# A convolution and quantized FFN kernel: half of the early PSUM evacuations move from VectorE to ScalarE and GpSimd, with new orders of work in the opening

## The chip, the cores and the metric

One core of one Trainium2 chip. The metric is device microseconds of the kernel, median over runs. A profile of one execution comes with it; its times are read from the start of the span.

## What is computed

`x` is 128 samples x 32 channels x 512 positions, float32. A grouped convolution along the positions (4 groups of 8 channels, 9 taps, padding 4) plus a shift per sample and channel gives `y`. Each token (one sample, one channel) is then a row of 512 values for a feed-forward block whose operands are all rounded to 8 bits with a scale per row:

```python
out = lax.conv_general_dilated(x, weight, (1,), [(4, 4)], feature_group_count=4, ...)
y = out + einsum('nd,od->no', c, c_weight)[:, :, None] + bias[None, :, None]
gate = qlinear(y, w_gate)          # 512 -> 1376, both operands rounded per row
up = qlinear(y, w_up)
h = silu(gate) * up
x = x + qlinear(h, w_down)         # 1376 -> 512
```

`qlinear` takes max|row|/127 as a scale for each token and each weight row, rounds, and multiplies back.

## The kernel before

The samples lie on the 128 partitions. One **tile** is one channel: 128 tokens; there are 32 tiles. Each engine runs a program of its own, in an order written out by hand; semaphores are the only ties.

**Convolution.** A group of 8 channels is computed in 8 **spans** of 64 positions (q = 0 to 31; q = 8g + i). `conv_span(q)` (L743) issues five float32 matmuls per span, each two passes in the trace: stationary a block of `x`, moving a table `toeplitz`. They add into one PSUM bank of 8 x 64 values. The first block covers 16 positions, the next three 24, and the last one 8, which the constant `LEAST = 16` widens to 16 with zero taps, so 128 columns. `add_shift(q)` (L585) on VectorE reads the bank, adds the shift and writes `y`; every second span `fold_y(q)` (L597) reduces two spans to maxima. After the 8 spans of a group `group_top/scale/inverse` give the token scales `x_scale` and `x_inv`.

**Weights.** Eleven tiles of 128 rows of gate and up weights (`load_w`): VectorE takes maxima (`weights_top`, L561), scales and inverses; GpSimd rounds (`round_w`, L389, two instructions per tile); TensorE transposes (`turn_gate_up`, L764); ScalarE copies out of PSUM (`copy_gate_up`, L472). The scales are spread over partitions by `turn_xq` (L782) and `copy_xq`. The inverses are made in pairs of tiles, so GpSimd rounds in pairs. `round_y(0)` and `round_y(1)` feed the first two tokens tiles through TensorE.

**Opening.** Spans 0 to 11 (`FRONT = 12`) and the eleven weight tiles are done before tile 0, interleaved on TensorE as span q, weight tile q - 2.

**The tile loop.** Gate and up have 1376 columns in pieces of 512, 512 and 352. For piece p of tile i: TensorE `gate_or_up`; VectorE `scale_gate(i,p)` (L662); ScalarE `silu(i,p)` (L518); GpSimd `scale_silu(i,p)` (L429); VectorE `multiply_up(i,p)` (L672), which also frees the PSUM bank of `up`. The orders within tile i:

- VectorE: scale_gate(i,0), multiply_up(i-1,2), scale_gate(i,1), token_scales(i-1), multiply_up(i,0), scale_down, scale_gate(i,2), add_shift, multiply_up(i,1), folds, weights_down.
- ScalarE: silu(i,0), silu(i,1), round_down, round_y, round_h(i-1), silu(i,2), convert_h(i-1).
- GpSimd: scale_silu(i,0), add_residual, scale_silu(i,1), convert_y (L411), convert_down (L402), scale_silu(i,2).
- TensorE: two gate pieces, one up piece, down(i-5), span, the other three pieces.

`SPANS_AT` places spans 12 to 15 in tiles 0 to 3 and the rest in tiles 5 to 12 and 17 to 20. `CHANNELS_AT` places the rounding of tokens; `w_down` is rounded in tiles 0 to 3. SyncE's queue (its order is that of the program) turns `hq` by DMA, loads slabs 2 and 3 of `x_blocks` in iterations 4 and 5, and behind them the first residuals (L299), for which `add_residual(0)` waits in tile 6.

Of the kernel before, what the change touches and what calls it, by code (L numbers as in the profile page):

```python
# [5 lines left out]
ALU = mybir.AluOpType  # L6
# [6 lines left out]
P = 128  # L13
# [11 lines left out]
def adaln_ffn(nc, x, x_blocks, cond_ctx_bias, taps_wide, w_gate_up, w_down, out):  # L25
# [17 lines left out]
    LEAST = 16  # L43
# [17 lines left out]
    with ExitStack() as ctx:  # L61
# [94 lines left out]


        def halves(bank):
# [13 lines left out]
        y_ready = sem("y_ready")  # L172
        y_part_ready = sem("y_part_ready")
# [50 lines left out]
                   ("scales", 2, 0), ("scales", 2, 1)]  # L224
        BY_PE = 2

        def use(kind, part, m):
            return XQ_USES.index((kind, part, m))

# [6 lines left out]
                       for first, c, n in ((0, BY_PE, CI - BY_PE), (4, 8, CI), (13, 16, CI), (21, 24, CI))  # L236
# [7 lines left out]


# [6 lines left out]
        def _(sp):  # L252
# [77 lines left out]
            load_w(0)  # L330
            load_x_piece(0)
            load_w(1)
            load_x_piece(1)
            load_w(2)
            load_w(3)
            load_x_piece(2)
            load_w(4)
# [4 lines left out]
            load_slab(1, 0)  # L342
            load_slab(1, 1)
            for o in range(KT):
                load_w_down(o)
# [34 lines left out]
        def _(pool):  # L380
# [58 lines left out]
            for i in range(TILES):  # L439
# [6 lines left out]
                for o in down_at(i - 1):  # L446
                    convert_down(o)
                scale_silu(i, 2)
# [4 lines left out]
        def _(act):  # L453
            act.dma_start(small_sb[:, :], cond_ctx_bias).then_inc(small_in, 16)
            act.dma_start(toeplitz[:, :, :, :].rearrange("p g c o -> p (g c o)"), taps_wide).then_inc(taps_in, 16)

            act.wait_ge(small_in, 16)
            act.activation(silu_trial[:, :], small_sb[:, 0:1], ACT.Silu)

# [20 lines left out]
            def copy_xq(n):  # L480
                kind, part, m = XQ_USES[n]
                act.wait_ge(xq_turned, n + 1)
                bank = xq_bank[n % 2]
# [12 lines left out]
            for j in range(5):  # L496
                copy_gate_up(j)
            copy_xq(0)
            copy_xq(1)
            copy_gate_up(5)  # L500
            copy_gate_up(6)
# [3 lines left out]
            copy_xq(2)  # L505
            copy_xq(3)
            copy_xq(4)
            copy_gate_up(8)
            copy_gate_up(9)
            copy_xq(5)  # L510
            copy_gate_up(10)
# [20 lines left out]
            for i in range(TILES):  # L532
# [6 lines left out]
                for n in CHANNELS_AT.get(i, []):  # L539
                    round_y(n)  # L540
                if i:
# [8 lines left out]
        def _(dve):  # L550
# [399 lines left out]
```

## Time and profile before

| | |
|---|---|
| median of 3 runs | 312.16 us (311.69 to 314.09) |
| profiled execution | 311.69 us, its span 309.9 us |
| mean granted TensorE clock | 0.994 |
| TensorE matmul busy | 286.2 us (92%) |
| VectorE busy | 257.2 us (83%) |
| ScalarE busy | 190.1 us (61%) |
| GpSimd busy | 187.2 us (60%) |

The busy times are sums over stages with different limits, so what a change of one stage is worth has to be read in that stage. TensorE's matmul time is modelled and includes the pipeline's tail.

### The profile page before, as it was taken

To read this page: it belongs to the slowest core of one execution; us is meant where nothing else is said; L and a number is where in the kernel's file an instruction comes from. 1 tells how busy PE (TensorE), PEld (TensorE's weight loads), DVE (VectorE), ACT (ScalarE), POOL (GpSimd) and SP (SyncE) were. 2 spreads that over 40 slices of the span, in tenths; PEclk is the share of its full clock that TensorE was granted. 3 is DMA by queue.
4 is the path that set the end of the run, shared out by engine and by line. 5 is a ranking of instruction groups with operands and counts; after the bars stand their busy time and mean duration, and the time that the engine had idled before them with its cause. 6 is when DMAs were issued, how large, how long until landed. Compare 5 with 4: busy or idle time off the path is not lost.

```text
span 309.9 us, 4607 instructions
## 1 busy us (share of the span) xinstructions
PE 286.2 (92%) x1575; PEld 168.3 (54%) x1575; DVE 257.2 (83%) x419; ACT 190.1 (61%) x217; POOL 187.2 (60%) x195
## 2 busy tenths in 40 slices
PE   0997878879799999999999999999999999999995
PEld 0987855444455555555444466566444444444543
DVE  1699669999886988897998869888988888888863
ACT  1044765797974856555688835445688866676750
POOL 1354528676745766556598855346587766666653
PEclk9999999979999999999999999999999999999999
DMA  7999503347999864443278983453366665424336
GB/s 274 419 399 401 241 1 79 76 99 160 314 364 182 192 156 114 114 109 94 75 149 228 296 218 101 104 84 101 85 151 175 164 175 124 81 80 111 86 82 215
DMA packets 80390, 51.71 MB, mean 167 GB/s; under 512 B 69520, under 2 KB 69904, under 8 KB 79472
## 3 DMA queue, kind: packets, MB, share of 16 engines
q1 hardware_dynamic: 80080, 50.80, 59.4%
q10 hardware_dynamic: 288, 0.62, 0.7%
q8 instruction: 12, 0.20, 0.3%
q14 instruction: 10, 0.08, 0.1%
HBM read 26.12 MB, written 8.39 MB: 111 GB/s over the span
## 4 chain that ended last, share of the span: by engine, by line
PE 63%; DVE 18%; DMA 6%; ACT 4%; issue 4%; POOL 3%; SPq 1%; DVEq 0%; POOLq 0%
PE bank L852 35%; PE bank L869 16%; PE bank L759 10%; DVE h_mem L672 4%; DMA xo_mem<-x 3%; DVE h_max L678 3%; DVE gu_max L564 3%; DMA slab<-x_blocks 2%; DVE y_part L601 2%; DVE sg_mem L662 2%; POOL sg_mem L429 2%; DVE y_mem L592 2%; DMA hq_mem<-hq_mem 1%; DVE d_max L580 1%; ACT wgu_t L476 1%
## 5 line engine op out<-in xcount | busy, mean ns | idle before, releaser
L852 PE MATMUL bank<-wgu_t,xq_mem 128*128 128x512 bf16 (+1 forms) x768 | 157.1, 360 | 9.3 <-DVE h_mem L672 6.9
L429 POOL TENSOR_TENSOR sg_mem<-sg_mem,gu_scale_row 128x512 f32<-128x512 f32 (+1 forms) x96 | 111.3, 1162 | 85.0 <-ACT sg_mem L518 84.7
L852 PEld LDWEIGHTS bank<-wgu_t,xq_mem 128*128 128x128 bf16 x768 | 74.7, 98 | 82.8 <-DVE h_mem L672 10.8
L518 ACT ACTIVATE sg_mem<-sg_mem,x_scale 128x512 f32<-128x512 f32 (+1 forms) x96 | 64.8, 676 | 65.6 <-DVE sg_mem L662 65.3
L662 DVE TENSOR_TENSOR sg_mem<-bank,gu_scale_row 128x512 f32<-128x512 f32 (+1 forms) x96 | 60.1, 627 | 23.5 <-PE bank L852 23.5
L869 PE MATMUL bank<-wd_t,hq_mem 128*128 128x512 bf16 (+1 forms) x341 | 78.2, 379 | 0.0
L672 DVE SCALAR_TENSOR_TENSOR h_mem<-bank,x_scale,sg_mem 128x512 f32<-128x512 f32 (+1 forms) x96 | 66.3, 691 | 7.7 <-POOL sg_mem L429 6.8
L523 ACT ACTIVATE h_mem<-h_mem,h_inv 128x1376 f32<-128x1376 f32 x32 | 46.1, 1441 | 21.0 <-DVE h_inv L557 21.0
L759 PE MATMUL bank<-toeplitz,slab 128*128 128x192 f32 (+1 forms) x320 | 52.7, 317 | 4.8 <-DMA slab<-x_blocks 4.8
L759 PEld LDWEIGHTS bank<-toeplitz,slab 128*128 128x128 f32 x320 | 51.3, 199 | 7.4 <-DMA toeplitz<-taps_wide 3.0
L869 PEld LDWEIGHTS bank<-wd_t,hq_mem 128*128 128x128 bf16 (+1 forms) x341 | 33.3, 98 | 40.2 <-issue 0.3
L678 DVE TENSOR_REDUCE h_max<-h_mem 128x1 f32<-128x1376 f32 x32 | 50.4, 1575 | 0.0
L530 ACT ACTIVATE hq_mem<-h_mem 128x1376 bf16<-128x1376 f32 x32 | 42.7, 1334 | 0.0
L437 POOL TENSOR_TENSOR xo_mem<-xo_mem,hq_mem 128x512 f32<-128x512 f32 x24 | 30.5, 1270 | 3.7 <-DMA xo_mem<-x 3.7
L690 DVE SCALAR_TENSOR_TENSOR hq_mem<-bank,h_scale,wd_scale_row 128x512 f32<-128x512 f32 x31 | 23.0, 743 | 3.7 <-PE bank L869 3.7
L476 ACT ACTIVATE wgu_t<-bank 128x1024 bf16<-128x1024 int16 (+1 forms) x11 | 11.0, 1003 | 20.8 <-PE bank L772 20.8
L394 POOL TENSOR_SCALAR hq_mem<-hq_mem,gu_inv 128x512 f32<-128x512 f32 (+1 forms) x14 | 9.4, 691 | 14.4 <-DVE gu_inv L576 14.3
L592 DVE TENSOR_TENSOR y_mem<-bank,shift 128x512 f32<-128x512 f32 x24 | 15.9, 679 | 1.2 <-PE bank L759 1.2
L464 ACT ACTIVATE y_mem<-y_mem,x_inv 128x512 f32<-128x512 f32 x24 | 15.8, 707 | 0.1
L564 DVE TENSOR_REDUCE gu_max<-hq_mem 128x2 f32<-128x1024 f32 (+1 forms) x7 | 8.4, 1203 | 7.5 <-DMA hq_mem<-w_gate_up 7.5
L601 DVE TENSOR_REDUCE y_part<-y_mem 128x8 f32<-128x1024 f32 x12 | 14.5, 1210 | 0.0
L411 POOL TENSOR_SCALAR yq_mem<-y_mem 128x512 bf16<-128x512 f32 x22 | 13.3, 617 | 1.6 <-ACT y_mem L464 1.1
(54 smaller groups left out, 108.1 us busy)
## 6 DMA issues: line engine op xcount, KB each, us to landing
xo_mem<-x SPq DMA_DIRECT2D x24, 256.0 KB, 3.0
out<-xo_mem SPq DMA_DIRECT2D x24, 256.0 KB, 2.0
slab<-x_blocks SPq DMA_DIRECT2D x3, 1088.0 KB, 7.7
hq_mem<-w_gate_up SPq DMA_DIRECT2D x6, 512.0 KB, 8.7
slab<-x_blocks SPq DMA_DIRECT2D x3, 1024.0 KB, 10.2
slab<-w_down SPq DMA_DIRECT2D x3, 688.0 KB, 7.8
h_mem<-w_gate_up SPq DMA_DIRECT2D x4, 512.0 KB, 13.9
slab<-x SPq DMA_DIRECT2D x1, 2048.0 KB, 9.1
```

Source lines behind the costliest of these rows:

```text
L429: pool.tensor_tensor(s, s, gu_scale_row[:, 1, at:at + n], ALU.mult).then_inc(silu_scaled, 1)
L437: pool.tensor_tensor(xo_of(i), xo_of(i), down_out[:, i % 2, :], ALU.add).then_inc(out_ready, 1)
L518: act.activation(s, s, ACT.Silu, scale=x_scale[:, i:i + 1]).then_inc(silu_done, 1)
L523: act.activation(hi, hi, ACT.Copy, bias=MAGIC, scale=h_inv[:, i:i + 1]).then_inc(h_rounded, 1)
L530: act.activation(hq[i % HQ_BUFS][:, 0:INTER], h[i % H_BUFS], ACT.Copy, bias=-MAGIC).then_inc(hq_ready, 1)
L662: dve.tensor_tensor(sg[i % SG_BUFS][:, at:at + n], gate_bank[(NP * i + p) % 2][:, 0:n], gu_scale_row[:, 0, at:at + n], ALU.mult).then_inc( ...
L672: dve.scalar_tensor_tensor(h[i % H_BUFS][:, at:at + n], up_bank[(NP * i + p) % 2][:, 0:n], x_scale[:, i:i + 1], sg[i % SG_BUFS][:, at:at + ...
L678: dve.tensor_reduce(h_max[:, one], h[i % H_BUFS], AX_X, ALU.max, apply_absolute_value=True)\
L690: dve.scalar_tensor_tensor(down_out[:, i % 2, :], down_bank[i % 2][:, :], h_scale[:, i:i + 1], wd_scale_row[:, :], ALU.mult, ALU.mult).the ...
L759: last = pe.matmul(out_span[:, :, lo:hi], slabs[g % 2][:, PER_SPAN * i + b, :], toeplitz[:, g, :, tap:tap + hi - lo], start=(b == 0), stop ...
L852: last = pe.matmul(bank[n % 2][:, 0:cols], xq_t[:, g, k, P * c:P * (c + 1)], wgu_t[:, m, k, at:at + cols], start=(k == 0), stop=(k == KT - 1))
L869: last = pe.matmul(down_bank[i % 2][:, :], hq_t[i % HQT_BUFS][0:r, j, :], wd_t[0:r, j, :], start=(j == 0), stop=(j == JT - 1))
```

## The change

- **Evacuation split.** Spans 2 to 5 and 8 to 15 (`BY_ACT`, twelve spans) are no longer evacuated by `add_shift`. ScalarE copies the bank to `y` (`copy_span`), GpSimd adds the shift in place (`shift_span`), and `fold_y` waits for GpSimd.
- **Placement.** GpSimd shifts spans 2, 3 after rounding weight tile 3, spans 4, 5 after tile 5, and spans 8 to 15 in tiles 0 to 4 ahead of `scale_silu(i,2)` (`SHIFTS_AT`). The folds of group 1 move to tiles 3 to 5 (`FOLDS_AT`), the tokens of group 1 from tiles 4 to 7 to tiles 6 to 9.
- **Opening.** TensorE's, VectorE's and ScalarE's orders are written out anew. Spans 8 to 11 come behind weight tile 7. Weight tile 10 and the last two spreads of scales move into tile 0, behind its first two gate pieces, which wait only for eight weight tiles.
- **Loads.** `w` tile 1 goes ahead of the first piece of `x`, other pieces change places; the taps are loaded in two parts, the second after weight tile 5 has landed; three of the four `w_down` tiles go ahead of the second half of slab 1.
- **Narrow last blocks.** `LEAST` is 8: the last block of each span has 64 columns in place of 128, and the table of taps shrinks by a quarter.

The core of the diff:

```diff
-    LEAST = 16
+    LEAST = 2 * PAD
+        BY_ACT = [2, 3, 4, 5] + list(range(SPANS, 2 * SPANS))
+        BY_DVE = [q for q in range(SLOTS) if q not in BY_ACT]
-                       for first, c, n in ((0, BY_PE, CI - BY_PE), (4, 8, CI), (13, 16, CI), (21, 24, CI))
+                       for first, c, n in ((0, BY_PE, CI - BY_PE), (6, 8, CI), (13, 16, CI), (21, 24, CI))
+        SHIFTS_AT = {0: [8], 1: [9], 2: [10, 11], 3: [12, 13], 4: [14, 15]}
+        FOLDS_AT = {3: [9, 11], 4: [13], 5: [15]}
+        def conv_bank_free(engine, q):
+            if q in BY_ACT:
+                engine.wait_ge(conv_copied, BY_ACT.index(q) + 1)
+            else:
+                engine.wait_ge(y_ready, BY_DVE.index(q) + 1)
...
+            load_w(1)
             load_x_piece(0)
-            load_w(1)
+            load_w(2)
             load_x_piece(1)
...
+            def shift_span(q):
+                g, i = divmod(q, SPANS)
+                span = y[g][:, :, SPAN * i:SPAN * (i + 1)]
+                pool.wait_ge(shift_ready, 1)
+                pool.wait_ge(conv_copied, BY_ACT.index(q) + 1)
+                pool.tensor_tensor(span, span, shift[:, CI * g:CI * (g + 1)].unsqueeze(2).broadcast_to([P, CI, SPAN]),
+                                   ALU.add).then_inc(y_shifted, 1)
+
             for j in range(JT):
                 round_w(j)
+                if j == 3:
+                    shift_span(2)
+                    shift_span(3)
+                elif j == 5:
+                    shift_span(4)
+                    shift_span(5)
...
                 for o in down_at(i - 1):
                     convert_down(o)
+                for q in SHIFTS_AT.get(i, []):
+                    shift_span(q)
                 scale_silu(i, 2)
...
+            act.wait_ge(w_tile_in[5], 16)
+            act.dma_start(toeplitz[:, 1:GROUPS, :, :]..., taps_wide[:, group_taps:]).then_inc(taps_rest_in, 16)
+            def copy_span(q):
+                g, i = divmod(q, SPANS)
+                act.wait_ge(conv_done, q + 1)
+                act.activation(y[g][:, :, SPAN * i:SPAN * (i + 1)],
+                               conv_bank(q)[:, :].rearrange("p (c l) -> p c l", c=CI), ACT.Copy).then_inc(conv_copied, 1)
...
# VectorE, the opening's new order
+            weights_inverse(0, 2)
+            weights_top(2)
             add_shift(0)
+            add_shift(1)
+            weights_top(3)
+            weights_scale(2, 2)
+            fold_y(1)
+            weights_inverse(2, 2)
+            weights_top(4)
+            weights_top(5)
+            weights_scale(4, 2)
+            fold_y(3)
+            weights_inverse(4, 2)
+            weights_top(6)
+            add_shift(6)
+            weights_top(7)
             add_shift(7)
+            weights_scale(6, 2)
+            fold_y(5)
+            weights_inverse(6, 2)
+            fold_y(7)
...
# TensorE, the opening's new order
+            turn_gate_up(0)
+            turn_gate_up(1)
+            conv_span(2)
+            conv_span(3)
+            turn_gate_up(2)
+            conv_span(4)
+            conv_span(5)
+            turn_gate_up(3)
+            turn_xq(0)
+            turn_xq(1)
+            conv_span(6)
+            conv_span(7)
+            turn_gate_up(4)
+            turn_gate_up(5)
+            turn_xq(2)
+            turn_xq(3)
+            turn_gate_up(6)
+            turn_gate_up(7)
+            turn_xq(4)
+            conv_span(8)
+            conv_span(9)
+            turn_gate_up(8)
+            conv_span(10)
+            turn_gate_up(9)
+            conv_span(11)
...
                 gate_or_up(i, 0, 1)
+                if i == 0:
+                    turn_gate_up(10)
+                    turn_xq(5)
+                    turn_xq(6)
                 gate_or_up(i, 1, 0)
```

ScalarE's new order in the opening is copies of weight tiles 0 and 1, spans 2 and 3, weight tiles 2 and 3, spans 4 and 5, scales, weight tiles 4 and 5, scales, weight tile 6, `round_y(0)` and `(1)`, weight tile 7, the first tokens, spans 8 and 9, then weight tiles 8, 9 and 10 among spans 10 and 11 and the last scales. In tiles 0 to 3 it copies spans 12 to 15 ahead of `round_h`.

## Rows read from the trace of the kernel before

**Rows 1.** Two stretches: busy us (instructions) by engine, clock, DMA share, GB/s.
```profile
60.00:80.00 20.00, 15.72 (x76) 8.03 (x77) 19.62 (x35) 17.00 (x20) 14.35 (x14) 0.91 0.68 154
...
99.00:146.00 47.00, 46.79 (x250) 27.51 (x251) 41.72 (x67) 27.62 (x30) 29.68 (x28) 1.00 0.52 130
```

**Rows 2.** Chain that ended last, 41 to 100 us: start us, us, what.
```profile
85.47 10.23 DMA xo_mem<-x
```

**Rows 3.** VectorE timeline, opening: start, us, engine, line, operation, count, idle before.
```profile
13.36 0.69 DVE L592 TENSOR_TENSOR y_mem<-bank,shift 128x512 f32<-128x512 f32 x1 [0.46 <-PE bank L759]
```

**Rows 4.** GpSimd timeline of the opening, same columns.
```profile
16.75 2.69 POOL L394 TENSOR_SCALAR hq_mem<-hq_mem,gu_inv 128x512 f32<-128x512 f32 x4 [2.15 <-DVE gu_inv L576]
...
21.65 2.69 POOL L394 TENSOR_SCALAR hq_mem<-hq_mem,gu_inv 128x512 f32<-128x512 f32 x4 [2.21 <-DVE gu_inv L576]
...
34.47 1.35 POOL L394 TENSOR_SCALAR hq_mem<-hq_mem,gu_inv 96x512 f32<-96x512 f32 x2
```

**Rows 5.** TensorE timeline of the opening, same columns.
```profile
7.79 6.95 PE L759 MATMUL bank<-toeplitz,slab 128*128 128x128 f32 x30 [2.85 <-DMA slab<-x_blocks]
...
28.39 1.69 PE L759 MATMUL bank<-toeplitz,slab 128*128 128x128 f32 x10 [1.96 <-DMA slab<-x_blocks]
...
34.49 0.62 PE L804 MATMUL bank<-ident_bf,y_mem 128*128 128x128 bf16 x8 [1.16 <-ACT gu_scale_row L486]
...
41.48 2.76 PE L852 MATMUL bank<-wgu_t,xq_mem 128*128 128x512 bf16 x12 [1.58 <-ACT gu_scale_row L486]
```

**Rows 6.** Groups by shape, first 70 us: busy us, mean ns, idle.
```profile
L429 POOL TENSOR_TENSOR sg_mem<-sg_mem,gu_scale_row 128x512 f32<-128x512 f32 x8 | 10.0, 1274 | 9.5 <-ACT sg_mem L518 9.5
...
L601 DVE TENSOR_REDUCE y_part<-y_mem 128x8 f32<-128x1024 f32 x4 | 4.8, 1212 | 0.0
...
L411 POOL TENSOR_SCALAR yq_mem<-y_mem 128x512 bf16<-128x512 f32 x6 | 3.7, 617 | 1.1 <-ACT y_mem L464 1.1
...
L486 ACT ACTIVATE gu_scale_row<-bank 128x512 f32<-128x512 f32 x4 | 2.2, 594 | 0.0
...
L796 PEld LDWEIGHTS bank<-ident,gu_scale 128*128 128x128 f32 x20 | 2.1, 137 | 0.0
```

**Rows 7.** ScalarE timeline: first two SiLUs, then the second of tiles 1 to 5.
```profile
43.77 1.34 ACT L518 ACTIVATE sg_mem<-sg_mem,x_scale 128x512 f32<-128x512 f32 x2 [2.34 <-DVE sg_mem L662]
...
52.05 0.72 ACT L518 ACTIVATE sg_mem<-sg_mem,x_scale 128x512 f32<-128x512 f32 x1 [0.36 <-DVE sg_mem L662]
...
60.98 0.72 ACT L518 ACTIVATE sg_mem<-sg_mem,x_scale 128x512 f32<-128x512 f32 x1 [0.37 <-DVE sg_mem L662]
...
68.79 0.72 ACT L518 ACTIVATE sg_mem<-sg_mem,x_scale 128x512 f32<-128x512 f32 x1 [0.37 <-DVE sg_mem L662]
...
76.50 0.72 ACT L518 ACTIVATE sg_mem<-sg_mem,x_scale 128x512 f32<-128x512 f32 x1 [0.37 <-DVE sg_mem L662]
...
83.11 0.72 ACT L518 ACTIVATE sg_mem<-sg_mem,x_scale 128x512 f32<-128x512 f32 x1 [0.52 <-DVE sg_mem L662]
```

**Rows 8.** GpSimd timeline, last SiLU product of tile 2.
```profile
66.23 0.94 POOL L429 TENSOR_TENSOR sg_mem<-sg_mem,gu_scale_row 128x352 f32<-128x352 f32 x1
```

**Rows 9.** VectorE timeline, the `up` product behind it.
```profile
67.58 0.57 DVE L672 SCALAR_TENSOR_TENSOR h_mem<-bank,x_scale,sg_mem 128x352 f32<-128x352 f32 x1
```

**Rows 10.** TensorE timeline of tiles 1 to 7.
```profile
54.62 3.36 PE L852 MATMUL bank<-wgu_t,xq_mem 128*128 128x352 bf16 x16 [1.43 <-DVE h_mem L672]
...
63.55 5.04 PE L852 MATMUL bank<-wgu_t,xq_mem 128*128 128x352 bf16 x16 [2.00 <-DVE h_mem L672]
...
99.21 1.04 PE L852 MATMUL bank<-wgu_t,xq_mem 128*128 128x512 bf16 x4 [0.73 <-DVE h_mem L672]
```

**Rows 11.** Groups by line and shape, 155 to 281 us.
```profile
L759 PEld LDWEIGHTS bank<-toeplitz,slab 128*128 128x128 f32 x80 | 12.0, 191 | 0.6
...
L759 PE MATMUL bank<-toeplitz,slab 128*128 128x192 f32 x48 | 9.1, 326 | 0.0
...
L759 PE MATMUL bank<-toeplitz,slab 128*128 128x128 f32 x32 | 5.5, 274 | 0.0
```

More of the change, by code:

```diff
@@ L342, in _ @@
             load_slab(1, 0)
+            for o in range(KT - 1):
+                load_w_down(o)
             load_slab(1, 1)
-            for o in range(KT):
-                load_w_down(o)
+            load_w_down(KT - 1)
             for i in range(TILES + 1):
@@ L494, in copy_down_row @@
                 act.activation(wd_scale_row[:, :], down_bank[1][:, :], ACT.Copy).then_inc(wd_row_copied, 1)
-            for j in range(5):
-                copy_gate_up(j)
+            copy_gate_up(0)
+            copy_gate_up(1)
+            copy_span(2)
+            copy_span(3)
+            copy_gate_up(2)
+            copy_gate_up(3)
+            copy_span(4)
+            copy_span(5)
             copy_xq(0)
             copy_xq(1)
+            copy_gate_up(4)
             copy_gate_up(5)
+            copy_xq(2)
+            copy_xq(3)
             copy_gate_up(6)
@@ L540, in _ @@
                     round_y(n)
+                for q in SPANS_AT.get(i, []):
+                    if q in BY_ACT:
+                        copy_span(q)
                 if i:
@@ L704, in _ @@
                 for q in SPANS_AT.get(i, []):
-                    add_shift(q)
+                    if q in BY_DVE:
+                        add_shift(q)
                 multiply_up(i, 1)
-                for q in SPANS_AT.get(i, []):
-                    if q % 2:
-                        fold_y(q)
+                for q in FOLDS_AT.get(i, []):
+                    fold_y(q)
                     if q % SPANS == SPANS - 1:
@@ L809, in turn_down_row @@
                 pe.wait_ge(d_scale_ready, KT)
-                pe.wait_ge(y_ready, FRONT)
+                pe.wait_ge(xq_copied, use("scales", 2, 1) + 1)
                 spread(down_bank[1], lambda t: d_scale[:, t:t + 1], KT).then_inc(wd_row_turned, 1)
@@ L846, in gate_or_up @@
                 else:
-                    pe.wait_ge(xq_copied, len(XQ_USES))
+                    pe.wait_ge(xq_copied, use("tokens", 0, 0) + 1)
+                    pe.wait_ge(w_copied, ROW_PARTS[p][1])
+                if n == 2:
                     pe.wait_ge(w_copied, JT)
@@ L860, in down @@
                         pe.wait_ge(wd_turned[b], 16 * KT // WDQ_BUFS)
-                    pe.wait_ge(y_ready, FRONT)
+                    pe.wait_ge(xq_copied, use("scales", 2, 0) + 1)
                 elif i == 1:
```

92 lines of the change are left out of this document (41 added, 51 removed).

## The prediction

> **What bounds the kernel now.** The table of stretches comes first: it says which engine is full where. From 99 us on TensorE is busy without a gap (46.79 of 47.00 us), while between 60 and 80 us it is VectorE that is full, 19.62 of 20.00 us, and GpSimd has 14.35 [rows 1]. So the run has three parts: an opening up to the first gate piece at 41.48 us [rows 5], tiles 0 to 4 with VectorE full, and from tile 5 on TensorE's own pace, which takes over each microsecond that the first two parts win or lose. Late in the second part the chain of waits leaves the engines: the first residual lands 10.23 us after its issue at 85.47 [rows 2], and TensorE stands still for 0.73 us before 99.21 because of it [rows 10]. Next the timelines of the opening, engine by engine, and then the SiLUs of the tiles, because the loop VectorE, ScalarE, GpSimd, VectorE shows in them as one beat per tile [rows 7].
>
> **Opening, what is removed.** VectorE gives up eight shifts (spans 2 to 5, 8 to 11) and two folds of 1.21 us (mean 1212 ns, [rows 6]) before tile 0. It gets a head start on the weights as well, since tile 1 now lands ahead of `x`. But it can't use it: `add_shift(1)` still stands ahead of `weights_top(3)`, and the second span ends when it did, because the first spans start on the first piece of `x` (7.79 us, [rows 5]; 512 KB of weights go ahead, some 400 KB of taps go behind, so the same time), and `add_shift(1)` at 13.36 was already waiting for TensorE [rows 3]. From there on the same four operations follow as before, so GpSimd gets the inverses of weight tiles 2 and 3 at about the 16.75 us of now [rows 4].
>
> **Opening, what is added.** From there each pair of weight tiles goes through a ring of waits: GpSimd rounds the pair (2.69 us, [rows 4]), then does two shifts; VectorE waits in `fold_y` for the second, folds (1.21), and only behind that stands `weights_inverse` of the next pair, for which GpSimd waits. The price of a shift is not in the trace. It is a two-input float32 operation of 512 elements; the nearest row is the SiLU product on the same engine with 1274 ns, started every 1.24 us; the one-input conversion has 617 ns [rows 6]. I take 1.24, because two inputs are what they share, and keep 0.62 as the lower end; nothing shows an upper end above 1.3. The ring is then 2.69 + 2.5 + 1.2 + 0.3 of handoffs = 6.7 us against 21.65 - 16.75 = 4.9 us now [rows 4]. Pair 4, 5 starts at 23.4, pair 6, 7 at 30.1, pair 8, 9 at 34.7 (behind `fold_y(7)`, the group's scales and two maxima), tile 10 ends at 38.8 where it now ends at 34.47 + 1.35 = 35.8 [rows 4].
>
> The Trainium skill (GPSIMD Engine Reference, The C++ chunk loop) says that both inputs of a two-input operation go through one read port, about 2.5 cycles per element at the least. The trace agrees, 1274 against 617 ns [rows 6]; by that page a broadcast second input saves nothing.
>
> TensorE turns weight tile 6 at 31.5, ScalarE copies it and rounds two channels, and the tokens are turned at 34.5, just as at 34.49 now [rows 5]. Behind this stand four spans, where two stood: 2 x 1.45 = 2.9 us more. Against them the wait of 1.58 us ahead of the first gate piece goes [rows 5], and weight tile 10 and two spreads (1.2 us) move behind it. First gate piece: 41.48 + 2.9 - 1.6 - 1.2 = 41.6. The first SiLU stands in ScalarE's queue behind the copies of what was moved: 41.6 + 1.7 (two gate pieces) + 1.2 + 1.7 (three copies with handoff) = 46.2, less 0.8 as the first copy starts while TensorE still spreads, so 45.4 against 43.77 [rows 7]. **Opening: +1.6 us.** ScalarE's eight copies of spans (594 ns each by the nearest PSUM copy, [rows 6]) lie in its idle time; without it they would cost 8 x 0.6 = 4.8. Its new wait for weight tile 5 holds up `copy_gate_up(0)` and all behind it by some 2 us; GpSimd asks for span 2 only after weight tile 3, so it costs nothing.
>
> **The clock.** In the new opening TensorE has nothing to do from 27.9 (scales spread) to 31.5 us (weight tile 6 rounded), then 0.9 us of transposes within 3 us, then the serial stretch that sets tile 0. Now it idles 1.96 us there [rows 5] and keeps its clock; but 2.00 us idle ahead of 63.55, in a stretch that was thin already, was followed by the lower level (1.2 GHz): the same 16 matmuls took 5.04 us in place of 3.36 [rows 10], +1.7 us. That drop was hidden by VectorE. Here it would be on the path. The idle time is nearly twice as long, so I count it: **+1.7 us**, bounds 0 and 3.4.
>
> **Tiles 0 to 4.** VectorE sheds four shifts (0.6 each) and its folds change places. GpSimd gets one, one, two, two and two shifts, each ahead of `scale_silu(i,2)`, and queued behind that on VectorE stand `multiply_up(i,2)`, then `scale_gate(i+1,1)`, `token_scales` and the rest; TensorE waits for the banks. So the beat counts. In tile 2 that product ends at 66.23 + 0.94 = 67.17 [rows 8] and VectorE takes it at 67.58 [rows 9]: 0.41 us of slack, for 2 x 1.24 = 2.5 us of new work, +2.05. The same reading of the other four tiles: tile 0, one shift against 0.35 slack and a ScalarE copy in the same queue, +1.15; tile 1, one shift against 1.55 slack, -0.2 (VectorE's saving shows); tile 3, two shifts against 1.6 slack, with two folds more on VectorE, +0.45; tile 4, two shifts, but two conversions of 0.6 leave GpSimd and ScalarE's `round_h` sets the end anyway, +0.15. **Sum +3.6 us**: the beats of now (44.40, 52.05, 60.98, 68.79, 76.50, 83.11; that is 7.65, 8.9, 7.8, 7.7, 6.6, [rows 7]) become 8.8, 8.7, 9.85, 8.15, 6.75. GpSimd is the bound in place of VectorE. At 0.62 per shift the sum would be +0.3, with VectorE the bound in tiles 3 and 4.
>
> **Tiles 5 on.** The residual's landing comes later by less than TensorE does, since slab 2 is out of its way by then: the 0.73 us [rows 10] goes, **-0.7**, bounds 0 and -0.7. The last fold of group 1 and its scales lengthen tile 5 to some 8.4 us of VectorE, no more than TensorE needs there (45 matmuls per tile, at 250 in 47.0 us [rows 1]: 8.46); its cost is 0, or 0.5 without that cover. The tokens of group 1 have two tiles of lead, cost 0.
>
> **Narrow last blocks.** 64 columns fewer save 326 - 274 = 52 ns per pass [rows 11], two passes, 0.105 us per span at most. But the next float32 weight load must be in by then. It has 191 ns [rows 11], a load with one spread column 137 [rows 6]: float32 loads of a full block are no shorter than the pass they hide under, so I let only the last pass of a span gain, and only where bf16 follows. That is twelve of the sixteen spans inside TensorE's stretch: **-0.65 us**, bounds 0 and -1.7. The Trainium skill (TensorE: Matmul & The Clock Gate, LDWEIGHTS) gives a load of 128 columns as 128/1.2 = 107 ns; by that rule the pass ahead of another float32 load gains nothing. No row shows a 64-column pass.
>
> **Sum.** 1.6 + 1.7 + 3.6 - 0.7 - 0.65 = +5.5 us on the profiled 311.69: 317.2. The median of the runs lies 0.47 above that execution, so 317.6.
>
> **Rivals.**
>
> 1. *The clock holds.* The same without 1.7: 315.9. For it: 1.96 us idle at 26.4 passed without a drop. Against: a longer gap.
> 2. *GpSimd's shift is cheap (0.62 us)*, a broadcast input costing like none. Ring 5.4 us, tokens turned 2.6 us earlier, the first SiLU 1.0 earlier than now; tiles +0.3; narrow blocks -0.65; the stall -0.1: 310.7. It decides below some 0.75 us per shift. Against: every two-input row of GpSimd.
> 3. *VectorE's relief comes through*, the other side. If the shifts fit GpSimd's idle 30 to 40% without ever being waited for, VectorE's twelve shifts of 0.6 come off a full engine: 312.2 - 7.2 - 0.65 = 304.3, less what TensorE takes up first, so 304 to 308. It decides where GpSimd's last SiLU product still ends before VectorE asks. Against: 0.41 us slack in tile 2.
> 4. *The split hangs on waits I placed too late*, 312 to 314: the opening turns even because the maxima run ahead, and only tile 2 loses.
>
> A measurement of this kernel tells 1% (3.1 us) from no change. Chances: forecast 0.37, rival 1 0.20, rival 2 0.13, rival 3 0.10, rival 4 0.20. Slower by over 1% means above 315.3: all of the forecast, most of rival 1: 0.53. Faster means below 309.0: rival 3 and a tail of 2: 0.15. Within: 0.32. The range leaves rival 3 and the far end of the bounds out: 309.5 to 319.8; the forecast's own is 316.3 to 319.5.
>
> **What would show it.** GpSimd's `shift_span` at 1.24 us; VectorE idle ahead of `fold_y(3)` and `fold_y(5)`, on GpSimd; rounding of pairs at 23.4 and 30.1 us; TensorE idle near 28 to 31.5 and a granted clock of 0.5 behind it; the first SiLU near 45.4 (47 with the drop); `multiply_up(2,2)` waiting for GpSimd some 2 to 3 us; the second SiLU of tile 5 near 88 to 90; a 10-pass span of 1.37 us where bf16 follows. A shift below 0.75 us, or VectorE with no idle time in tiles 2 and 3, would make me wrong.

## The result and the profile after

The changed kernel takes 316.63 us, the median of five runs (314.99 to 317.34), against 312.16 before: ratio 1.0116, 95% interval 1.0074 to 1.0158. It is slower, as forecast, by 1.2% in place of 1.7% (the two medians lie 1.4% apart). The profiled execution is the quickest of the five (314.99 us, span 313.2), so against the profiled one before it is 3.3 us longer.

The page's busy times and slices come first.

```profile
PE 287.7 (92%) x1575; PEld 168.4 (54%) x1575; DVE 252.0 (80%) x407; ACT 195.8 (63%) x229; POOL 199.5 (64%) x207
...
PEclk9999799979899999999999999999999999999999
```

VectorE lost 5.2 us of work and GpSimd gained 12.3, and the kernel is longer: a busy time that falls on a full engine is no gain when what it waits for comes later. The clock's row has three slices below 9, where that of before had one:

```profile
PEclk9999999979999999999999999999999999999999
```

The stretches of the changed kernel show where they lie (busy us and instructions by engine, clock, DMA share, GB/s).

```profile
30.00:41.00 11.00, 9.20 (x78) 8.88 (x77) 6.06 (x11) 7.73 (x10) 5.16 (x8) 0.84 0.56 232
...
60.00:80.00 20.00, 16.05 (x80) 8.47 (x78) 16.36 (x27) 15.43 (x19) 16.58 (x17) 0.91 0.55 116
80.00:99.00 19.00, 16.87 (x80) 9.06 (x80) 16.53 (x29) 11.45 (x15) 10.40 (x10) 0.91 1.11 330
```

VectorE is no longer full between 60 and 80 us: 16.36 us where it had 19.62 [rows 1]. Now the opening, first GpSimd's timeline, to be held against [rows 4].

```profile
16.12 2.71 POOL L415 TENSOR_SCALAR hq_mem<-hq_mem,gu_inv 128x512 f32<-128x512 f32 x4 [5.37 <-DVE gu_inv L638]
18.79 2.05 POOL L442 TENSOR_TENSOR y_mem<-y_mem,shift 128x512 f32<-128x512 f32 x2
22.27 2.70 POOL L415 TENSOR_SCALAR hq_mem<-hq_mem,gu_inv 128x512 f32<-128x512 f32 x4 [1.44 <-DVE gu_inv L638]
24.94 2.04 POOL L442 TENSOR_TENSOR y_mem<-y_mem,shift 128x512 f32<-128x512 f32 x2
28.42 2.70 POOL L415 TENSOR_SCALAR h_mem<-h_mem,gu_inv 128x512 f32<-128x512 f32 x4 [1.44 <-DVE gu_inv L638]
32.95 2.71 POOL L415 TENSOR_SCALAR h_mem<-h_mem,gu_inv 128x512 f32<-128x512 f32 x4 [1.83 <-DVE gu_inv L638]
```

The pairs of weight tiles are rounded from 16.12, 22.27 and 28.42 us on: the ring of 6.15 us. The idle time of 1.44 us before the second and third pair is on the inverse, which VectorE hasn't issued yet, as its timeline shows.

```profile
20.87 1.22 DVE L666 TENSOR_REDUCE y_part<-y_mem 128x8 f32<-128x1024 f32 x1 [2.02 <-POOL y_mem L442]
22.00 0.17 DVE L638 RECIPROCAL gu_inv<-gu_scale 128x4 f32<-128x4 f32 x1
```

`fold_y(3)` waits 2.02 us for GpSimd's shift, and the reciprocal behind it is what GpSimd waits for. TensorE's timeline of the opening and of the start of its own stretch, against [rows 5, 10]:

```profile
29.84 0.62 PE L842 MATMUL bank<-ident_bf,h_mem 128*128 128x128 bf16 x8 [1.63 <-POOL h_mem L415]
...
32.88 1.01 PE L877 MATMUL bank<-ident_bf,y_mem 128*128 128x128 bf16 x8 [1.08 <-ACT y_mem L512]
33.69 3.96 PE L829 MATMUL bank<-toeplitz,slab 128*128 128x128 f32 x20
...
41.23 1.89 PE L939 MATMUL bank<-wgu_t,xq_mem 128*128 128x512 bf16 x8
```

```profile
82.33 5.05 PE L939 MATMUL bank<-wgu_t,xq_mem 128*128 128x352 bf16 x16 [2.13 <-DVE h_mem L740]
...
89.60 1.53 PE L829 MATMUL bank<-toeplitz,slab 128*128 128x128 f32 x10
...
104.00 2.54 PE L956 MATMUL bank<-wd_t,hq_mem 128*128 128x512 bf16 x11
```

The same two places in TensorE's timeline of before:

```profile
79.10 3.36 PE L852 MATMUL bank<-wgu_t,xq_mem 128*128 128x352 bf16 x16 [2.03 <-DVE h_mem L672]
...
100.08 2.54 PE L869 MATMUL bank<-wd_t,hq_mem 128*128 128x512 bf16 x11
```

Spans 8 and 9 take 3.96 us from the first start to the last end (3.01 in experiments 2 to 4), and the 16 matmuls at the start of TensorE's stretch (82.33) 5.05 us where the same ones of before took 3.36. Part of each lies at the lower clock: the granted clock is 0.74 from 33.7 to 37.5 us and 0.65 from 82.3 to 87.2, where it was 1.00 over the 3.4 us from 79.0 of before. The SiLUs, against [rows 7]:

```profile
44.90 1.34 ACT L577 ACTIVATE sg_mem<-sg_mem,x_scale 128x512 f32<-128x512 f32 x2
```

```profile
54.01 0.72 ACT L577 ACTIVATE sg_mem<-sg_mem,x_scale 128x512 f32<-128x512 f32 x1 [1.64 <-DVE sg_mem L730]
...
62.52 0.72 ACT L577 ACTIVATE sg_mem<-sg_mem,x_scale 128x512 f32<-128x512 f32 x1 [1.08 <-DVE sg_mem L730]
...
72.02 0.72 ACT L577 ACTIVATE sg_mem<-sg_mem,x_scale 128x512 f32<-128x512 f32 x1 [2.08 <-DVE sg_mem L730]
...
79.74 0.72 ACT L577 ACTIVATE sg_mem<-sg_mem,x_scale 128x512 f32<-128x512 f32 x1 [0.49 <-DVE sg_mem L730]
...
86.90 0.72 ACT L577 ACTIVATE sg_mem<-sg_mem,x_scale 128x512 f32<-128x512 f32 x1 [0.99 <-DVE sg_mem L730]
```

The beats are 8.5, 9.5, 7.7 and 7.2 us between tiles 1 and 5. From the first SiLU to the second one of tile 5 it is 42.0 us, before 39.3. The product behind GpSimd's shifts in tile 2, against [rows 8, 9]:

```profile
67.76 2.04 POOL L442 TENSOR_TENSOR xq_mem<-xq_mem,shift 128x512 f32<-128x512 f32 x2
69.76 2.17 POOL L464 TENSOR_TENSOR sg_mem<-sg_mem,gu_scale_row 128x352 f32<-128x352 f32 x2
```

```profile
70.80 0.58 DVE L740 SCALAR_TENSOR_TENSOR h_mem<-bank,x_scale,sg_mem 128x352 f32<-128x352 f32 x1 [2.20 <-POOL sg_mem L464]
```

Two shifts end at 69.80, the product of 352 columns follows, and VectorE has been idle for 2.20 us when it can take it.

The account of the profiled span: TensorE's stretch begins 3.23 us later (82.33 against 79.10), of which 1.13 stand at the first SiLU (44.90 against 43.77). Its first 16 matmuls add 1.69. The wait of 0.73 us [rows 10] is gone; from start to start it had cost 0.90 (9.34 from one `down` to the next, now 8.39 with a span 0.05 shorter). With that and two narrow spans the changed kernel is 3.92 us behind when the third `down` of the stretch starts (104.00 against 100.08). Of these 0.64 are won back up to the last `down`: 0.54 by ten gains of 0.05 from the narrow blocks, 0.10 by a shorter last wait.

### The profile page after: what moved, and what is told of

It is laid out like the page before. It is cut to its first block, busy times and chain, and to the rows that moved or that the text cites. A ratio compares the mean times of both kernels' runs of the same rounds, so it can differ in the third digit from the quotient of the medians.

```text
span 313.2 us, 4635 instructions
## 1 busy us (share of the span) xinstructions
PE 287.7 (92%) x1575; PEld 168.4 (54%) x1575; DVE 252.0 (80%) x407; ACT 195.8 (63%) x229; POOL 199.5 (64%) x207
## 3 DMA queue, kind: packets, MB, share of 16 engines
HBM read 25.99 MB, written 8.39 MB: 110 GB/s over the span
## 4 chain that ended last, share of the span: by engine, by line
PE 68%; DVE 11%; POOL 8%; ACT 5%; issue 5%; DMA 3%; SPq 0%; DVEq 0%; POOLq 0%
PE bank L939 36%; PE bank L956 17%; PE bank L829 12%; POOL sg_mem L464 4%; DVE h_max L746 2%; DVE h_mem L740 2%; DMA slab<-x_blocks 2%; DVE sg_mem L730 2%; DVE y_part L666 1%; DMA hq_mem<-hq_mem 1%; POOL xq_mem L442 1%; ACT sg_mem L577 1%; PE bank L842 1%; ACT h_mem L582 1%; DVE y_mem L654 1%
## 5 line engine op out<-in xcount | busy, mean ns | idle before, releaser
L939 PE MATMUL bank<-wgu_t,xq_mem 128*128 128x512 bf16 (+1 forms) x768 | 159.2, 362 | 9.3 <-DVE h_mem L740 8.7
L829 PE MATMUL bank<-toeplitz,slab 128*128 128x192 f32 (+2 forms) x320 | 51.3, 314 | 2.9 <-DMA slab<-x_blocks 2.9
L654 DVE TENSOR_TENSOR y_mem<-bank,shift 128x512 f32<-128x512 f32 x20 | 13.3, 681 | 2.5 <-PE bank L829 2.5
```

The source lines that it names most:

```text
L829: last = pe.matmul(out_span[:, :, lo:hi], slabs[g % 2][:, PER_SPAN * i + b, :], toeplitz[:, g, :, tap:tap + hi - lo], start=(b == 0), stop ...
L939: last = pe.matmul(bank[n % 2][:, 0:cols], xq_t[:, g, k, P * c:P * (c + 1)], wgu_t[:, m, k, at:at + cols], start=(k == 0), stop=(k == KT - 1))
```

## The experiments

Each kernel is the changed one with one edit, unless said otherwise. Ratios are to the kernel before, run beside it; the changed kernel's is 1.0116, so 0.001 is 0.31 us. Differences from the changed kernel go by these ratios; its own, of five runs, is known to 1.3 us to each side.

Two things differ between executions of one kernel, and every profile below is one execution. One is the start: GpSimd's rounding of weight tiles 2 and 3, from which the ring runs, began at 16.12 us in the changed kernel's profile and at 15.88 to 17.10 in those of the experiments with the same opening up to there. The other is the clock: beside the experiments, 27 executions of the kernel before with a mean granted clock of 0.989 took 313.1 us on the average, and 29 with 0.993 or 0.994 took 311.7.

**1. The shifts of the tiles behind the last product.**

```diff
-                for q in SHIFTS_AT.get(i, []):
-                    shift_span(q)
                 scale_silu(i, 2)
+                for q in SHIFTS_AT.get(i, []):
+                    shift_span(q)
```

> The changed kernel with the eight shifts of tiles 0 to 4 behind the last SiLU product of their tile on GpSimd. Theory (the queue order: a shift ahead of that product holds up VectorE's up product): the waits of 1.2, 1.2 and 2.2 us go, the beats of the second SiLU fall from 8.5, 8.5, 9.5, 7.7 to about 7.7, 7.6, 7.6, 7.6, so the profiled span falls by 3 us, to 310.2 or below before. Rival A (the GpSimd work itself is too much, wherever it stands): within 1 us of the changed kernel. Rival B (only the lower TensorE clock costs): beats fall, but the time follows the number of clock drops alone.

Ratio 1.0028 (0.9999 to 1.0057): 2.7 us faster than the changed kernel with all its shifts still done. From the first SiLU to the second one of tile 5 it is 39.2 us, as before. ScalarE's timeline:

```profile
46.62 1.34 ACT L577 ACTIVATE sg_mem<-sg_mem,x_scale 128x512 f32<-128x512 f32 x2
...
54.74 0.72 ACT L577 ACTIVATE sg_mem<-sg_mem,x_scale 128x512 f32<-128x512 f32 x1 [0.65 <-DVE sg_mem L730]
...
62.65 0.72 ACT L577 ACTIVATE sg_mem<-sg_mem,x_scale 128x512 f32<-128x512 f32 x1 [0.49 <-DVE sg_mem L730]
...
70.56 0.72 ACT L577 ACTIVATE sg_mem<-sg_mem,x_scale 128x512 f32<-128x512 f32 x1 [0.49 <-DVE sg_mem L730]
...
85.80 0.72 ACT L577 ACTIVATE sg_mem<-sg_mem,x_scale 128x512 f32<-128x512 f32 x1 [0.98 <-DVE sg_mem L730]
```

That first SiLU is 1.7 us later than the changed kernel's: 1.0 because this execution started later, and 0.7 by a longer stretch at the lower clock in the opening.

```profile
17.10 2.71 POOL L415 TENSOR_SCALAR hq_mem<-hq_mem,gu_inv 128x512 f32<-128x512 f32 x4 [6.44 <-DVE gu_inv L638]
```

So its span, 312.0 us, hides part of the gain, and I missed the 310.2. Rival A is out: elsewhere in the queue the same work costs nothing against before, though VectorE's relief of four shifts doesn't show either. Rival B is out as well for the beats: both profiles have a granted clock of 0.982 and the drop at tile 5, and the beats fall. It is not out for the whole of the 2.7 us, since the runs of this kernel have clocks of 0.982 to 0.989 and those of the changed one 0.973 to 0.982; at 0.982 two runs took 313.7 us on the average and the one of the changed kernel 314.99. The first beats are near 7.9 us, 0.2 to 0.4 longer than I wrote.

**2. The inverses ahead of the folds.**

```diff
-            fold_y(3)
             weights_inverse(4, 2)
+            fold_y(3)
...
-            fold_y(5)
             weights_inverse(6, 2)
+            fold_y(5)
```

> The changed kernel with weights_inverse ahead of fold_y(3) and fold_y(5) in the opening. Theory (the ring of waits in the opening, GpSimd shift, fold, inverse, GpSimd rounding): pairs of weight tiles are rounded every 4.8 us (2.7 + 2.0 + handoff) in place of 6.15, the tokens are turned 1.5 to 2.5 us earlier than at 32.9, the first SiLU near 42.5 in place of 44.9: 2 us faster. Rival (TensorE's own work in the opening is what counts, the fold's wait is hidden): 0 to 0.5 us.

Ratio 0.9995 (0.9966 to 1.0024), 3.8 us faster: nearly twice what I expected of an exchange of two neighbours. GpSimd's and ScalarE's timelines:

```profile
20.57 2.72 POOL L415 TENSOR_SCALAR hq_mem<-hq_mem,gu_inv 128x512 f32<-128x512 f32 x4
...
26.37 2.70 POOL L415 TENSOR_SCALAR h_mem<-h_mem,gu_inv 128x512 f32<-128x512 f32 x4 [1.08 <-DVE gu_inv L638]
```

```profile
41.53 1.34 ACT L577 ACTIVATE sg_mem<-sg_mem,x_scale 128x512 f32<-128x512 f32 x2
```

The pair 4, 5 starts at 20.57, without any wait behind the shifts, and pair 6, 7 at 26.37. The first SiLU is at 41.53, 3.4 us ahead of the changed kernel's: 2.0 by the ring (tokens turned at 30.85), of which 0.2 lie in the start of this execution, and 1.3 because the tokens' transposes and spans 8 and 9 now find the high clock (3.01 us for the spans). The drop at tile 5 stays (5.05 us for the 16 matmuls). The rest of the 3.8 is within the intervals.

**3. and 4. Matmuls without use in TensorE's idle time.** Seventeen float32 ones in the opening (experiment 3), and the same with eight bf16 ones per tile in tiles 0 to 4 (experiment 4):

```diff
+            def keep_busy(n):
+                for _ in range(n):
+                    pe.matmul(banks[6][:, 0:P], ident[:, :], ident[:, :], start=True, stop=True)
...
+            pe.wait_ge(conv_copied, 3)
+            keep_busy(4)
             turn_xq(2)
             turn_xq(3)
+            keep_busy(6)
             turn_gate_up(6)
+            keep_busy(3)
             turn_gate_up(7)
+            keep_busy(4)
             turn_xq(4)
...
                 gate_or_up(i, 1, 1)
+                if i == 0:              # from here on experiment 4 only
+                    pe.wait_ge(xq_copied, use("scales", 2, 0) + 1)
+                if i < LAG:
+                    for _ in range(8):
+                        pe.matmul(down_bank[0][:, :], xq_t[:, 0, 0, 0:P], wgu_t[:, 0, 0, 0:512], start=True, stop=True)
                 gate_or_up(i, 1, 2)
```

> The changed kernel with 17 float32 matmuls without use put into TensorE's idle time between 26 and 33 us; they write a bank that the next span overwrites. Theory (the lower clock at 33 to 36 us comes from that idle time and is on the path): granted clock 1.00 up to 41 us, spans 8 and 9 in 2.8 in place of 3.8 us, first SiLU 1.0 us earlier, time 1 us lower. Rival (the drop is hidden, or comes whatever TensorE does): same time within 0.3 us.

> The same, and in tiles 0 to 4 eight more bf16 matmuls without use (1.7 us) ahead of the last up piece, where TensorE waits about 2 us. Theory: no stretch at the lower clock after 41 us either, tile 5's 16 matmuls in 3.4 in place of 5.05 us: 2.7 us faster than the changed kernel in all, and runs closer together (their clocks now differ from 0.973 to 0.982). Rival (tiles 0 to 4 are bound by GpSimd and VectorE so that a slower TensorE is hidden): no faster than with the opening alone.

Ratios 1.0029 (0.9998 to 1.006) and 1.0000 (0.9973 to 1.0026). In the first the spans 8 and 9 take 3.01 us, and with the tokens' transposes 1.3 us are won. This execution started 0.56 us later (16.68 in place of 16.12), and the extra matmuls put nothing off, so the first SiLU is at 44.14, 0.8 us earlier. The profiled spans differ by 1.2 us (312.0), since 0.7 of the lead of 1.9 at the first `down` is lost in the wait for the last turned `hq` (0.95 us in place of 0.24). The ratios differ by more: 2.7 us, with intervals of 1.0 and 1.3 us to each side. The stretch in which TensorE takes over, by its timeline in experiment 4:

```profile
33.67 3.01 PE L829 MATMUL bank<-toeplitz,slab 128*128 128x128 f32 x20
...
81.36 3.36 PE L948 MATMUL bank<-wgu_t,xq_mem 128*128 128x352 bf16 x16 [0.41 <-DVE h_mem L740]
```

```profile
core 0: 310.5 us, clock 1.000
```

16 matmuls in 3.36 us, and the granted clock is 1.000 over the whole run. The beats of tiles 1 to 4 stay what they were (8.5, 9.5 and 7.7 us), and only the one that ends in tile 5 falls, from 7.2 to 6.5 (43.91 to 85.23: 41.3 us in all), so the clock and GpSimd's queue are two costs and not one. The twelve runs lie within 311.45 to 312.96, the five of the changed kernel within 314.99 to 317.34 at clocks of 0.973 to 0.982; a stretch that adds 1.7 us, like that at tile 5, takes 0.0055 from the mean over 313 us. Which of these stretches fall on the path differs from run to run: the profile of experiment 3 has one at 55.82 us, where it was hidden, one at 73.84, where it cost 0.5 us (a beat of 8.3 in place of 7.7), and none at tile 5. With the tiles' idle time left as it is, a drop stands at tile 5 in the profiles of experiments 1, 2, 5, 9 and 11, and only earlier in those of 3, 6 and 8.

**5. VectorE takes spans 8 to 15 back.**

```diff
-        BY_ACT = [2, 3, 4, 5] + list(range(SPANS, 2 * SPANS))
+        BY_ACT = [2, 3, 4, 5]
...
-        SHIFTS_AT = {0: [8], 1: [9], 2: [10, 11], 3: [12, 13], 4: [14, 15]}
+        SHIFTS_AT = {}
...
-            copy_span(8)
-            copy_span(9)
             copy_gate_up(8)
-            copy_span(10)
             copy_gate_up(9)
-            copy_span(11)
...
             for o in down_at(-1):
                 weights_down(o)
+            for q in range(8, 12):
+                add_shift(q)
```

> The changed kernel with spans 8 to 15 evacuated by VectorE again: 8 to 11 behind its last weight work in the opening, where it now idles 6 us, 12 to 15 in tiles 0 to 3 as before; spans 2 to 5 stay split, the folds stay where the change put them. Theory (GpSimd's shifts ahead of the last product are what tiles 0 to 4 pay for): beats of the second SiLU 7.7, 7.8 to 8.0, 7.8, 8 to 9, 6.5 and the tiles 2 to 2.7 us shorter in sum. Rival A (VectorE is so full that its shifts cost as much as GpSimd's): no change within 1 us. Opening unchanged within 0.5 us by both, apart from clock drops.

Ratio 1.0040 (1.0019 to 1.0061), 2.4 us faster; 39.8 us from the first SiLU to the second of tile 5, beats 7.8, 7.8, 8.2 and 7.6. It has a drop at tile 5 too, as TensorE's timeline says:

```profile
79.97 5.04 PE L937 MATMUL bank<-wgu_t,xq_mem 128*128 128x352 bf16 x16 [2.03 <-DVE h_mem L738]
```

Against experiment 1 (39.2 us) this prices VectorE's own relief once GpSimd's queue is in order, in one execution of each: 0.6 us for four shifts, less than the 2.4 us they last. By their ratios the two kernels are 0.4 us apart, within the intervals.

**6. 128 columns again in the last block.**

```diff
-    LEAST = 2 * PAD
+    LEAST = 16
```

> The changed kernel with the last block of each span 128 columns wide again (and the table of taps as large as before). Theory (the last pass of a span gains only where a bf16 matmul follows): a span of ten passes 1.42 us again in place of 1.37, 2.84 in place of 2.79 for a pair, so the profiled span 0.6 us longer, within what a measurement tells. Rival (both passes of 64 columns gain): 0.105 us per span, 1.7 us longer. Rival (the loads gain too, by the smaller table): the first span starts later by over 0.3 us.

Ratio 1.0164 (1.0141 to 1.0187), 1.5 us slower than the changed kernel, but the two intervals overlap, so the time can't tell the 0.6 us of the theory from the 1.7 of the rival. The lengths can. Two spans in a row, by TensorE's timelines of the changed kernel and of this one:

```profile
185.07 2.95 PE L829 MATMUL bank<-toeplitz,slab 128*128 128x128 f32 x20
```

```profile
186.61 3.00 PE L829 MATMUL bank<-toeplitz,slab 128*128 128x128 f32 x20
```

A pair gains 0.05 us, as much as a single span (1.53 in place of 1.58), so the span that is followed by float32 gains nothing and the rival is out. The passes, in the groups by shape from 155 to 281 us of the changed kernel and of this one (busy us, mean ns, idle):

```profile
L829 PE MATMUL bank<-toeplitz,slab 128*128 128x64 f32 x16 | 2.6, 247 | 0.0
```

```profile
L829 PE MATMUL bank<-toeplitz,slab 128*128 128x128 f32 x32 | 5.5, 274 | 0.0
```

The 247 ns are a mean of two kinds of record: the first pass of a narrow block has 219 ns, and the second starts 56 ns behind it (273 and 109 with 128 columns); the second pass has 275 ns at either width, and bf16 follows 111 or 112 ns behind its start. Ahead of a float32 span the first pass of that span takes the 0.05 us again (165 ns to the next start in place of 112). So the gain shows in the first pass of the block and not in the last, and is kept only where bf16 follows.

**7. The narrow blocks alone**, on the kernel before.

> The kernel before with the narrow last blocks alone. Theory: ten passes of a span in 1.37 in place of 1.42 us where bf16 follows, in the sixteen spans inside TensorE's stretch and nowhere else on the path: 0.65 us faster at most, which a measurement hardly tells; taps that are a quarter smaller start the first span up to 0.3 us earlier. Rival (both passes gain): 1.7 us faster.

Ratio 0.9957 (0.9928 to 0.9985): 1.3 us faster. The first SiLU is at 43.13 in place of 43.77, but most of that is there before the opening's spans can have given it:

```profile
16.23 2.69 POOL L394 TENSOR_SCALAR hq_mem<-hq_mem,gu_inv 128x512 f32<-128x512 f32 x4 [2.36 <-DVE gu_inv L576]
```

Weight tiles 2 and 3 are rounded from 16.23 us on in place of 16.75 [rows 4], which a smaller table of taps may have given or the execution's luck. Behind the tokens' transposes only two spans are left, 0.1 us. TensorE's timeline shows a single span of 1.53 us in place of 1.58 from first start to last end.

```profile
81.67 2.54 PE L869 MATMUL bank<-wd_t,hq_mem 128*128 128x512 bf16 x11
```

The first `down` starts at 81.67, before at 82.29; the last one 1.70 us ahead of before's. In between are the twelve gains of 0.05 us (0.65, as worked out) and 0.4 by a shorter wait for the residual (0.29 us in place of 0.73). The measured 1.3 us has an interval that holds my 0.65, and the rival's 1.7 it doesn't exclude by itself, but the spans' length does (0.05 each, not 0.105).

**8. A full second input for the shift** (y + y in place of y + shift, so the shift itself is left out of the result).

```diff
-                pool.tensor_tensor(span, span, shift[...].unsqueeze(2).broadcast_to([P, CI, SPAN]),
+                pool.tensor_tensor(span, span, span,
```

> The changed kernel with the shift's broadcast operand replaced by the span itself (y + y in place of y + shift for the twelve spans; this part of the result is left wrong). It asks why a shift took 1.02 us where the SiLU product of the same size takes 1.24. Theory (a second input that is read from one address per channel is cheaper): 1.24 us each, and the time 1.5 to 2.5 us longer, since GpSimd's additions are on the path. Rival (the three-dimensional pattern or the in-place add makes it cheaper): 1.02 us again and no change in time.

Ratio 1.0156 (1.0131 to 1.0181), no slower than the changed kernel beyond the intervals, and the groups by shape up to 90 us, of the changed kernel and of this one, say why:

```profile
L442 POOL TENSOR_TENSOR xq_mem<-xq_mem,shift 128x512 f32<-128x512 f32 x8 | 8.2, 1043 | 0.0
```

```profile
L442 POOL TENSOR_TENSOR xq_mem<-xq_mem 128x512 f32<-128x512 f32 x8 | 8.2, 1040 | 0.0
```

1040 ns with two full inputs, 1043 with the broadcast one. My theory fell: the broadcast is not what makes the shift cheaper than a product of the same size.

**9. Both reorderings**, the edits of experiments 1 and 2 together.

> The changed kernel with both reorderings: GpSimd's shifts behind the last product of a tile, and weights_inverse ahead of fold_y(3) and fold_y(5). Theory (two separate places, so the gains add): 3.8 + 2.7 = 6.5 us faster than the changed kernel, near 310.2, 0.7% below before, less what a clock drop at tile 5 (1.7 us) takes back. Rival (one hidden behind the other, or behind the loads of slabs 2, 3 and the residuals): no better than the better one alone, 312.

Ratio 0.9908 (0.9888 to 0.9928), 309.57 us: the gains add (6.5 us by the ratios, as expected). TensorE's timeline still has the drop at tile 5:

```profile
76.94 5.05 PE L939 MATMUL bank<-wgu_t,xq_mem 128*128 128x352 bf16 x16 [2.03 <-DVE h_mem L740]
```

**10. The same with the matmuls without use in tiles 0 to 4.**

> The kernel with both reorderings, and eight bf16 matmuls without use per tile in tiles 0 to 4 ahead of the last up piece. Theory (the drop to the lower clock at tile 5 is on the path, 5.05 in place of 3.36 us for 16 matmuls, and follows from the idle time of tiles 0 to 4): granted clock 1.00 throughout, tile 5's matmuls in 3.4, 1.5 us faster than without, near 308.0. Rival (with VectorE the bound in tiles 0 to 4, the extra matmuls delay the last up piece): no change or slower by up to 1 us.

Ratio 0.9884 (0.9858 to 0.9911), 309.1 us. TensorE's timeline shows tile 5's 16 matmuls, and the last `down` of all; under it is the same last row of experiment 9:

```profile
77.24 3.35 PE L939 MATMUL bank<-wgu_t,xq_mem 128*128 128x352 bf16 x16
```

```profile
301.46 2.58 PE L998 MATMUL bank<-wd_t,hq_mem 128*128 128x256 bf16 x22 [1.08 <-DMA hq_mem<-hq_mem]
```

```profile
301.99 2.58 PE L993 MATMUL bank<-wd_t,hq_mem 128*128 128x256 bf16 x22 [0.23 <-DMA hq_mem<-hq_mem]
```

The 16 matmuls take 3.35 us, and the `down` of each tile starts 1.4 us ahead of experiment 9's (80.43 against 81.82 for the first). The last one starts only 0.5 us ahead: in the tail TensorE is not the bound, and it waits 1.08 us for the turned `hq` where it waited 0.23. So the 1.5 us I expected are there until the tail and 0.5 us at its end; the intervals of the two kernels overlap. Two of experiment 9's six runs had a clock of 1.000 without any such matmuls, and took 308.26 and 308.73 us.

**11. The product of GpSimd in the shift's pattern**, on the kernel of experiment 9.

```diff
-                pool.tensor_tensor(s, s, gu_scale_row[:, 1, at:at + n], ALU.mult)
+                s3 = s.rearrange("p (c l) -> p c l", c=CI)
+                pool.tensor_tensor(s3, s3, gu_scale_row[:, 1, at:at + n].rearrange("p (c l) -> p c l", c=CI), ALU.mult)
```

> The kernel with both reorderings and the SiLU product of GpSimd addressed as 8 rows of 64 (or 44) in place of 512 (352) elements in a row; the same elements. It asks why a shift takes 1.04 us and a product of the same size 1.27. Theory (the pattern in two dimensions is what makes it cheaper, since a shift with a full second input took 1.04 as well): 1.04 us a product, 5 to 8 us of GpSimd's busy time gone in all, total time at most 1 us lower as GpSimd is hidden for most of the run. Rival (the buffers, or the pattern is merged back when it is built): 1.27 again and no change.

Ratio 0.9877 (0.985 to 0.9904), no different from experiments 9 and 10. The product's row is what it was:

```profile
L465 POOL TENSOR_TENSOR sg_mem<-sg_mem,gu_scale_row 128x512 f32<-128x512 f32 x33 | 42.1, 1277 | 26.8 <-ACT sg_mem L579 26.8
```

The trace's own records say why: the product's operands stand there as one row of 512 elements (`[512,1,1]`), as in the other kernels, and the shift's as 8 rows of 64 (`[64,8,1]`). The pattern was merged back, the second rival, and this tried nothing new about the time.

## Why the prediction was right

**The ring of the opening** was right as a mechanism, and experiment 2 shows it: with the two instructions exchanged its first turn takes 4.7 us and the second 5.8, with 0 and 1.08 us of waiting. Its size was off by one term, the price of a shift: 1.02 us from start to start against my 1.24, so 6.15 us per turn against 6.7. I had 0.62 and 1.3 as ends and went by the nearest row, which was the wrong one by 0.2. Two turns of it make 1.1 us. The second span was done 0.6 us earlier than I took from [rows 3], which is luck of this execution: in the other profiles with this opening the ring starts 0.2 us earlier to 1.0 later. Together they had the tokens turned at 32.9, not 34.5. The first SiLU came 1.13 us later, of which the clock has 1.3: without it the opening of this execution would have cost nothing, not 1.6.

**The clock** came as forecast in the opening, and cost 1.3 us there, not 1.7. That the idle time brings it is shown by experiment 3, and by the profiles at large: the eight transposes of the tokens take 1.01 us in all five with this opening's waits (the changed kernel, experiments 1, 5, 6 and 8) and 0.61 in all six where the idle time is filled or shortened (experiments 2, 3, 4, 9, 10, 11). But the shape I gave was wrong: no gap of 3.6 us, but four of 1.14, 1.63, 0.72 and 1.08 between 26.0 and 32.9, none as long as the 1.96 of before or the 2.70 us of experiment 7 that passed without a drop. I compared the longest gap. The four together make 4.6 us; in experiment 2, where the clock held, they make 2.8. What I left out is the second drop, at tile 5, at the very place where TensorE takes over: 1.69 us in the profile, and gone in experiment 4. I had said of a drop in the tiles that VectorE hides it, going by the one at 63.55 [rows 10]; a hidden drop and one on the path differ only by which tile they fall in. The change is not its only cause: by their clocks, 0.005 lower, nearly half of the executions of the kernel before have one such stretch more than its profile, and are 1.5 us longer.

**Tiles 0 to 4**: +3.6 forecast; measured +2.1 up to the start of TensorE's stretch (3.23 less 1.13), +2.7 up to the second SiLU of tile 5, which already waits for TensorE at the lower clock. The order of the waits was right (experiments 1 and 5); the size was off by the same term: the first four beats (8.5, 8.5, 9.5, 7.7) came out 0.3, 0.2, 0.35 and 0.4 us below mine, with one, one, two and two shifts in them of 0.22 us less each. The two shifts of tile 4 cost nothing. The idle times I read are there: 1.2, 1.2 and 2.2 us ahead of `multiply_up(i,2)` in tiles 0 to 2.

**The residual's wait** went, -0.7 forecast and -0.9 from start to start. **The narrow blocks** gave 0.05 us at each of twelve places in TensorE's stretch, 0.65 as worked out, and for the reason given (only where bf16 follows), though the records show it in the first narrow pass and not in the last.

**The sum**, +5.5 against +3.3 in the profile, is the balance of errors of both signs: opening 1.8 and tiles 1.5 too dear, the clock 1.3 too cheap (3.0 in two drops), the last two terms 0.3 too small. That the total came within 1 us of the measured median is in part luck. The 0.47 us between the profiled execution and the median was a poor guide as well: the changed kernel's median lies 1.64 above its profiled execution, with clocks of 0.973 to 0.978 in the other four runs and 0.982 in it.

**The signs.** Those of the mechanism are there: GpSimd's waits for the inverse, the lower clock behind the idle time (0.50 from 32.8 to 33.6 us), `multiply_up(2,2)` waiting 2.2 us, a span of ten passes that is 0.05 us shorter. The places were all too late, for the reasons above: the shift at 1.02 us and not 1.24, the pairs at 22.27 and 28.42 and not 23.4 and 30.1, the first SiLU at 44.90 and not 47, the second of tile 5 at 86.90 and not 88 to 90. The wait ahead of `fold_y(5)` that I named doesn't show as idle time of VectorE.

**The rivals.** The cheap shift (0.62) is out by its row. The relief of VectorE (rival 3) was locked up by an order of two queues: with both orders turned round the kernel takes 309.57 us, 0.9% less than before by its ratio. Only part of that is relief, since the narrow blocks and the shorter residual's wait give 1.5 us of it; in the profile of experiment 9 the first SiLU is 1.35 us earlier than before's and the tiles up to 5 are 0.5 shorter.

## What to carry to other kernels

Work moved from a full engine to one that idles 40% is free only at a place of its queue where nobody waits for what stands behind it: read the slack of the very next result, not the engine's idle share. The same holds for a wait: what stands behind it on its own queue is what it costs. And idle time of TensorE in a stretch where it is not the bound can bring the lower clock into the stretch where it is, a few us later: in the opening it came behind four gaps, each shorter than ones that had passed without it. A profile is one execution; look at the clocks of all runs before a difference of 1 or 2 us is put down to the change.

## What I had not expected of the hardware

- A GpSimd add of 8 rows of 64 elements, float32, two inputs, took 1.04 us, whether the second input was a broadcast or a full one; the product and the residual's add of 512 elements in a row took 1.27. Experiment 8 excludes the broadcast. The pattern stays the likeliest cause: the residual's add is the same operation, in place and float32, and differs from the one of experiment 8 in the pattern and in that its two inputs are different buffers. No run shows it, since in experiment 11 the pattern was merged back to one row.
- Matmuls without use pay for themselves: 17 in the opening and 40 in the tiles took the granted clock from 0.973 to 0.982 up to 0.998 to 1.000, and the time down by 3.6 us by the ratios.
- Two passes of 64 columns in place of 128 gain 0.05 us where bf16 follows and nothing where float32 does, against 0.105 by the columns alone. The Trainium skill (TensorE: Matmul & The Clock Gate, LDWEIGHTS) gives a load of 128 columns as 107 ns, an estimate by which a shorter pass ahead of another float32 load gains nothing. The trace agrees in the sum (a pair of spans takes 2.95 us in place of 3.00, one gain and not two), though a single narrow pass is followed by the next one after 56 ns.
